# Layer normalisation on one core: variance and its root held once per token on a quarter of the partitions, then spread by four matmuls

## The reference, cut to what matters

```python
m = mean(x, axis=-1)
v = mean((x - m) ** 2, axis=-1)
y = (x - m) / sqrt(v + 1e-5)
```

## Time and profile before

| | us |
|---|---|
| median of 3 runs (4844.75 to 4852.0) | 4845.29 |
| the profiled execution, its own time | 4846.32 |
| its span in the profile | 4844.7 |
| PE busy | 4509.8 (93%) |
| DVE busy | 3645.8 (75%) |
| ACT busy | 3157.8 (65%) |
| POOL busy | 541.7 (11%) |
| mean granted TensorE clock | 0.962 |

### The profile page before, as it was taken

One profiled execution on the slowest core, in us unless ns is written; L12 is line 12 of the kernel. 1 busy time (PEld: TensorE's weight loads), 2 busy tenths in 40 slices (PEclk: granted clock), 3 DMA queues, 4 the chain that ended last, 5 costly groups with the idle time before them and its releaser, 6 DMA issues. The chain is left out here.

```text
span 4844.7 us, 107645 instructions
## 1 busy us (share of the span) xinstructions
PE 4509.8 (93%) x36227; PEld 2729.0 (56%) x36227; DVE 3645.8 (75%) x3699; ACT 3157.8 (65%) x5605; POOL 541.7 (11%) x1382
## 2 busy tenths in 40 slices
PE   6599999999999999999999969999885799999999
PEld 4344444444444444444444447777654478888887
DVE  4599999899999999999999956555355554444444
ACT  3158888788888888888888834444464454444444
POOL 4501111111111111111111100000000000000000
PEclk8789999999999999999999979999998899999999
DMA  5611110200202012012122220010001300000000
GB/s 174 190 29 21 24 28 18 34 18 18 34 18 34 19 21 35 18 31 65 39 56 45 44 88 28 25 35 9 27 17 48 123 14 9 13 13 13 13 4 14
DMA packets 217985, 182.41 MB, mean 38 GB/s; under 512 B 128032, under 2 KB 167632, under 8 KB 216448
## 3 DMA queue, kind: packets, MB, share of 16 engines
q1 hardware_dynamic: 201152, 167.99, 14.0%
q0 software_dynamic: 16384, 8.42, 0.7%
HBM read 120.47 MB, written 71.89 MB: 40 GB/s over the span
## 5 line engine op out<-in xcount | busy, mean ns | idle before, releaser
L894 DVE TENSOR_REDUCE PM<-A 128x2 f32<-128x1024 f32 x2092 | 2457.2, 1220 | 97.3 <-PE A L781 64.9
L871 ACT ACTIVATE PR<-SB 128x512 f32<-128x512 f32 x4100 | 2121.1, 603 | 367.2 <-PE SB L794 354.6
L814 PE MATMUL PV<-PR,VH 128*32 128x256 f32 x16384 | 1293.4, 387 | 3.5 <-issue 3.5
L781 PE MATMUL A<-QST,KA 48*128 48x512 f32 x4184 | 1196.4, 476 | 67.0 <-DMA QF<-QFD 40.8
L814 PEld LDWEIGHTS PV<-PR,VH 128*32 128x32 f32 x16384 | 433.2, 110 | 557.9 <-issue 367.0
L781 PEld LDWEIGHTS A<-QST,KA 48*128 48x128 f32 x4184 | 428.7, 187 | 525.1 <-issue 457.8
L794 PE MATMUL SB<-KST,QST 50*128 50x512 f32 x3075 | 689.8, 411 | 5.1 <-ACT PR L871 4.6
L794 PEld LDWEIGHTS SB<-KST,QST 50*128 50x128 f32 x3075 | 387.9, 187 | 213.3 <-ACT PR L871 209.3
L2045 DVE TENSOR_TENSOR m_h_lo<-m_h_full,m_h_hi 128x512 fp32r<-128x512 f32 x320 | 221.6, 693 | 276.5 <-ACT m_h_hi L1945 276.2
L802 PE MATMUL SB<-KF,QF 99*32 99x512 bf16 x4100 | 414.9, 384 | 1.2 <-ACT PR L871 1.2
L1939 ACT ACTIVATE m_h_full<-m_h,constants 128x512 f32<-128x512 f32 x320 | 219.6, 686 | 255.4 <-PE m_h L69 254.2
(11 more groups left out here) (280 smaller groups left out, 5503.6 us busy)
## 6 DMA issues: line engine op xcount, KB each, us to landing
QST<-QS SPq DMA_DIRECT2D x54, 256.0 KB, 9.0
KA<-KAD SPq DMA_DIRECT2D x402, 32.0 KB, 1.8
KST<-KS SPq DMA_DIRECT2D x402, 32.0 KB, 1.9
QS<-parts SPq DMA_DIRECT2D x16, 512.0 KB, 5.6
KS<-parts SPq DMA_DIRECT2D x16, 512.0 KB, 4.7
KAD<-dealt SPq DMA_DIRECT2D x16, 512.0 KB, 3.3
m_x<-X3T SPq DMA_DIRECT2D x16, 512.0 KB, 3.8
moe_w_lo<-W SPq DMA_DIRECT2D x16, 512.0 KB, 10.0
```

The lines of the kernel that those rows point to most:

```text
L781: return nc.tensor.matmul(A[:, u % 2 * 2 + e, :], keys, QST[rows, slot, j * TB:(j + 1) * TB], start=True, stop=True)
L814: mm = nc.tensor.matmul(PV[at:at + 2 * HD, 0:HB], VH[:, slot, e, c, :], PR[:, (2 * c + e) % P_SLOTS, b * HB:(b + 1) * HB], start=(c == 0), ...
L871: nc.scalar.activation(PR[:, v % P_SLOTS, :], SB[:, s_bank(v), :], ACT.Exp, scale=SCALE).then_inc(s_free, 1)
L894: nc.vector.tensor_reduce(PM[:, par, :, i, j:j + 1], A[:, u % 2 * 2:u % 2 * 2 + 2, :], AX.X, ALU.max).then_inc(a_free, 1)
```

## The change

The variance matmul is cut in four groups of 128 tokens. Group g uses only 32 columns of the matrix of 1/256 and writes partitions 32g to 32g+31, columns 0 to 127, of the bank. So one 128x128 tile holds the variances of all 512 tokens, each on 32 partitions. Root and reciprocal work on that tile. Four matmuls with a 128x128 selection (a column of `quarter`, which has a 1 at partition 32g, taken 128 times) then write the factor of each token to all partitions, over the same bank, and the scale reads it from PSUM. The new step (tensor_spread) needs a semaphore and a place in TensorE's order; in qkv0 and ffn0 other places move too.

```diff
-        self.std = self.sq[:, 0, :]
+        self.std = self.sq[:, 0, 0:P]
     def tensor_var(self, pe, i):
         pe.wait_ge(self.squared, count(i + 1))
         for k in range(KC):
-            mm = self.nc.tensor.matmul(self.var_ps, self.ones[:, :], self.sq[:, k, :],
-                                       start=(k == 0), stop=(k == KC - 1))
+            for g in range(TT):
+                rows = slice(g * P // TT, (g + 1) * P // TT)
+                mm = self.nc.tensor.matmul(self.var_ps[rows, 0:P], self.ones[:, 0:P // TT],
+                                           self.sq[:, k, g * P:(g + 1) * P], start=(k == 0), stop=(k == KC - 1))
         mm.then_inc(self.var_ready, 1)
+    def tensor_spread(self, pe, i):
+        pe.wait_ge(self.rstd_ready, count(i + 1))
+        for g in range(TT):
+            mm = self.nc.tensor.matmul(self.var_ps[:, g * P:(g + 1) * P], self.quarter[:, g:g + 1].to_broadcast([P, P]), self.std,
+                                       start=True, stop=True)
+        mm.then_inc(self.spread, 1)
-    def vector_reciprocal(self, dve, i, half):
+    def vector_reciprocal(self, dve, i):
         dve.wait_ge(self.std_ready, count(i + 1))
-        std = self.std[:, half * (TB // 2):(half + 1) * (TB // 2)]
-        self.nc.vector.reciprocal(std, std).then_inc(self.rstd_ready, 1)
+        self.nc.vector.reciprocal(self.std, self.std).then_inc(self.rstd_ready, 1)
     def vector_scale(self, dve, i):
-        dve.wait_ge(self.rstd_ready, count(i * 2 + 2))
-        rstd = self.std.unsqueeze(1).to_broadcast([P, KC, TB])
+        dve.wait_ge(self.spread, count(i + 1))
+        rstd = self.var_ps.unsqueeze(1).to_broadcast([P, KC, TB])
     def scalar_std(self, act, i, eps):
-        self.nc.scalar.activation(self.std, self.var_ps, ACT.Sqrt,
+        self.nc.scalar.activation(self.std, self.var_ps[:, 0:P], ACT.Sqrt,
...
# setup, POOL: quarter is one memset and one affine_select more
# qkv0, PE: spread between values 0 and values 1; ahead of the loop after turn(1)
-                    for pair in range(TT // 2):
-                        values(i, slot, pair)
+                    values(i, slot, 0)
+                    if following:
+                        ln.tensor_spread(pe, i + 1)
+                    values(i, slot, 1)
# qkv0, DVE
-                        for part in range(2):
-                            ln.vector_reciprocal(dve, i + 1, part)
-                        ln.vector_scale(dve, i + 1)
-                    low(i, slot, 3)
+                        ln.vector_reciprocal(dve, i + 1)
+                    low(i, slot, 3)
+                    if following:
+                        ln.vector_scale(dve, i + 1)
+                    values(i, 0)
                     if following:
                         ln.vector_lo(dve, i + 1, 1 - slot)
-                    values(i, 0)
                     values(i, 1)
# ffn0, PE, ACT, DVE (chunk: piece)
-  {9: "projection", 11: "mean", 14: "variance", 22: "gate"}
+  {9: "projection", 12: "mean", 16: "variance", 20: "spread", 25: "gate"}
-  {6: "o_hi", 13: "square", 15: "std", 20: "hi"}
+  {6: "o_hi", 15: "square", 18: "std", 22: "hi"}
-  10: "x1", 12: "centre", 16: "reciprocal0", 18: "reciprocal1", 19: "scale", 21: "lo", 23: "gate"
+  10: "x1", 13: "centre", 18: "reciprocal", 20: "scale", 22: "lo", 23: "gate"
# qkv1, PE: spread after queries/keys 3, ahead of the values
# out1, PE: spread of both slots after both variances; DVE: both reciprocals, then both scales
# moe, PE: spread at c == 21 (mean 12, variance 16 as before); DVE: one reciprocal at c == 19, scale at 22 as before
```

More of the change, by code:

```diff
@@ L253, in _ @@
                 nc.gpsimd.memset(K["eps"][:, :], EPS).then_inc(consts, 1)
-                pool.wait_ge(zeroed, 1)
+                nc.gpsimd.memset(K["quarter"][:, :], 0.0).then_inc(zeroed, 1)
+                pool.wait_ge(zeroed, 2)
                 nc.gpsimd.affine_select(out=ident[:, :], in_=ident[:, :], compare_op=ALU.not_equal,
@@ L257, in _ @@
                                         channel_multiplier=1).then_inc(consts, 1)
+                nc.gpsimd.affine_select(out=K["quarter"][:, :], in_=K["quarter"][:, :],
+                                        compare_op=ALU.not_equal, fill=1.0, base=0,
+                                        pattern=[[-(P // TT), TT]], channel_multiplier=1)
             @block.tensor
@@ L1115, in front @@
                         ln.tensor_var(pe, j)
+                    elif part == "spread":
+                        ln.tensor_spread(pe, j)
                     elif part == "gate":
@@ L1151, in blocks @@
                         if following:
-                            front(i + 1, 1 - slot, {9: "projection", 11: "mean", 14: "variance", 22: "gate"}.get(c))
-                for part in ("projection", "mean", "variance"):
+                            front(i + 1, 1 - slot, {9: "projection", 12: "mean", 16: "variance", 20: "spread",
+                                                             25: "gate"}.get(c))
+                for part in ("projection", "mean", "variance", "spread"):
                     front(0, 0, part)
@@ L1226, in front @@
                         ln.vector_centre(dve, j, slot)
-                    elif part in ("reciprocal0", "reciprocal1"):
-                        ln.vector_reciprocal(dve, j, int(part[-1]))
+                    elif part == "reciprocal":
+                        ln.vector_reciprocal(dve, j)
                     elif part == "scale":
@@ L1263, in blocks @@
                                 1: "den0", 2: "den1", 3: "den2", 4: "den3", 5: "quotient", 7: "o_lo",
-                                10: "x1", 12: "centre", 16: "reciprocal0", 18: "reciprocal1", 19: "scale",
-                                21: "lo", 23: "gate"}.get(c))
+                                10: "x1", 13: "centre", 18: "reciprocal", 20: "scale",
+                                22: "lo", 23: "gate"}.get(c))
                     dve.wait_ge(h_free, count((i + 1) * C + RING))
@@ L1287, in _ @@
                 weights.lo(dve, 1)
-                for part in ("reciprocal0", "reciprocal1", "scale"):
+                for part in ("reciprocal", "scale"):
                     front(0, 0, 0, part)
@@ L1435, in _ @@
                 ln.vector_centre(dve, 0)
-                for part in range(2):
-                    ln.vector_reciprocal(dve, 0, part)
+                ln.vector_reciprocal(dve, 0)
                 ln.vector_scale(dve, 0)
@@ L1655, in blocks @@
                     for s in SLOTS:
-                        for part in range(2):
-                            ln[s].vector_reciprocal(dve, i, part)
+                        ln[s].vector_reciprocal(dve, i)
+                    for s in SLOTS:
                         ln[s].vector_scale(dve, i)
```

39 lines of the change are left out of this document (24 added, 15 removed).

## The result

The changed kernel takes 4765.43 us (median of 5 runs, 4762.52 to 4768.82) against 4845.29 for the kernel before on the same chip: ratio 0.9829, 95% interval 0.9818 to 0.984. The profiled execution has a span of 4763.8 us against 4844.7.

| stage | before | after | measured | forecast |
|---|---|---|---|---|
| setup and qkv0 | 205.3 | 186.5 | -18.8 | -16 |
| attention | 2597.2 | 2589.6 | -7.6 | 0 |
| ffn0 | 660.2 | 638.0 | -22.2 | -13 |
| qkv1 | 146.3 | 133.4 | -12.9 | -2 |
| keys and values of the second attention | 46.7 | 47.1 | +0.4 | 0 |

A forecast was written before the change was run, and what follows sets the result against it. PE was taken to bound ffn0 and moe, a chain through the engines qkv0 and out1, with qkv1 between. Terms -16-13-2-19+0 = -50 from 4845.3 gave 4795 us, range 4783 to 4808 (8 in 10: 4776 to 4820).

The forecast's parts named there:

- the two kinds of price: Change priced as PE work in ffn0, qkv1 and moe, as chain length in qkv0, out1 and each stage's first block.
- small matmuls do overlap: Denies the rival that small matmuls don't overlap: variance 1.8 us, +1.05 on 20 PE-bound blocks, total 4820; chance 0.25.
- out1 keeps its clock of 0.77: Denies the rival that more clock comes back, in qkv0 and part of out1 (8 us more): 4781; chance 0.12.
- PE does not stand at the spread: Denies the rival that the spread blocks PE's in-order queue, 3 us in each of 28 blocks: slower, 4879; chance 0.05.
- only half the overlap: 1.2: Variance on 32-column weights: 1.2 us instead of 1.72, bounds 0.6 and 1.8.
- the net of a block: Block that PE bounds: spread 0.9, variance -0.5, change of width 0.1, net +0.5 us.
- the first chains: First blocks of qkv0, ffn0, qkv1, moe: one chain through reciprocal, root, variance and spread, -1.7 us each.
- the 0.55 that I gave it: Drains by the skill's rule: two per normalisation, at most 0.55 us per block, 11 us over 20 PE-bound blocks.
- 2.1 a block: ffn0: PE's waits for f_x and ln_lo go with the later places; -2.1+0.5 = -1.6 a block, stage -13.
- the wait of 5.2: qkv1: ln_lo wait of 7.0 us in 6 times, 5.2 of it once; 0.36 a block gained, +0.5 paid: 0.
- 4.9 sooner: out1: shorter reciprocals bring lo 0 4.9 us sooner; taken as -4.8 in each of 4 iterations, -19.
- moe 0 and qkv0 -16: moe: first chain -1.7, block 0 -1.3, six others +0.5 each, sum 0; qkv0: 7 x -2.0 -1.7 = -16.

The follow-up runs named there:

- variance_grouped: The changed kernel with the variance's two loops exchanged, so four instructions in a row go to the same quarter of the array; 4760.78 us.
- gate_later: The kernel before with one place moved: in ffn0 TensorE's gate from chunk 22 to 25; ratio 0.9979.
- places_only: The kernel before with the new places in ffn0 and qkv0 and none of the new operations; 4836.91 us, ratio 0.999.
- operations_only: The changed kernel with the places of before in ffn0 and qkv0; 4784.23 us, ratio 0.9873.
- out1_filled: The changed kernel with filler matmuls in out1, 4 behind the two variances and 12 behind the two spreads, each iteration; 4756.7 us, ratio 0.9817.

## Why the prediction was right and wrong

- **Direction and the two kinds of price**: right. The change pays as PE work in some stages and as a shorter chain in the others; reciprocal 0.95, scale unchanged and spread 0.9 held, the root took 0.37 instead of 0.27. The order of the stages did not hold: out1 was to give most and ffn0 gave most. The rivals fell: small matmuls do overlap (a block of moe takes 127.6 us instead of 127.7, where that rival wanted 1.5 more), out1 keeps its clock of 0.77, and PE does not stand at the spread where it is the bound (no wait of PE at all in ffn0's steady blocks).
- **"The two instructions of one fp32 matmul go to the same quarter, so I expect only half the overlap: 1.2"**: this step failed. Measured 0.58, just under the lower bound of 0.6: four instructions run at a time, the full overlap, and variance_grouped shows that the order of the quarters in the program has no part in it. With 0.2 around it instead of 0.1 the net of a block is -0.05, not +0.5: 20 blocks x 0.55 = 11 us of the 31 that were missing. The same term was wrong in the first chains, where I took 0.8 off the variance: in moe the root starts 1.15 us behind the variance's start instead of 3.82, in qkv1 0.7 instead of 3.0. On the change of width, the Trainium skill, "TensorEngine Tiling (Array Packing)", Key Properties, says that another tiling mode drains the engine; the 0.09 us ahead of the variance agrees with it in kind, and even with the 0.11 behind it the price is under half of the 0.55 that I gave it.
- **"PE stands 1.3 us for f_x and 0.8 for ln_lo: 2.1 a block"**: mis-sized, since I took the idle figure for the price. By gate_later a wait costs 0.27 more, twice a block, 7 blocks: 4 us in ffn0. In qkv1 I also took the wait of 5.2 for the main part of the earlier trace rows and the short ones, 0.2 to 0.4 each, for small; each costs 0.4 to 0.6 from start to start and they are gone: the period went from 15.5 to 14.7. 0.8 x 7 = 6. Of the other 7 us of qkv1 the first stretch, to the first reciprocal, has 3.9 (variance from 3.0 to 0.7, root 0.3, and, by chance, a load that landed 1.3 sooner: this stretch, 14.8 before, is 14.1 and 15.7 in gate_later and places_only), the rest the shorter chains of the first and the last normalisation.
- **Attention, "I let it only shift"**: put at 0 because it has no normalisation. The stage is 54% of the span; its steps answer to the place of the code (4.6 us of the 7.6), and nothing in the rows of before could have told that.
- **"out1: 4.9 sooner"**: 3.2 to 3.7 measured (from first reciprocal to first reciprocal 31.9, 31.4, 30.1 before and 28.8, 27.9, 26.4 after). The spreads were taken as 0.9 each; at half clock they take 1.9, so scale starts 3.1 us behind the first reciprocal instead of the 2.0 that the prediction's times give. The price at half clock stood in the prediction; the stage's sum didn't use it.
- **moe 0 and qkv0 -16**: moe's first chain gave 3.2 instead of 1.7 us and block 0 2.9 instead of 1.3, the other six the 0.55 above. In qkv0 the mechanism (low 3 in the time of the spread, part of the clock back) came as described, -18.8; places_only shows that the same order without the short reciprocal loses 10.7. That the sum comes within 3 us says little of its terms, since the stage scatters by 3 from kernel to kernel.
- **The size as a whole**: the misses of ffn0 (9), qkv1 (11), moe (6.5), attention (8) and qkv0 (3) point the same way, and out1's 6 the other.

## What to carry to other kernels

Read a wait of TensorE from start to start and not from the idle figure, and add what the first matmul behind it takes longer. When a change adds or removes instructions, compare the stages that it does not touch before crediting it with the sum: here 4.6 us of 80 came from the place of the code; 40 idle matmuls took them off the kernel before as well and put 14 us on the ninth and tenth steps of the changed one. Read a time that agrees with its forecast stage by stage as well: in operations_only and in out1_filled the sum was right and the terms were not. Try the places and the operations of a change apart: an order that pays with the new operations can lose without them.

## What was unexpected

- 16 fp32 instructions with 32-wide weights and 128 columns take 0.58 us, and another 16 behind them 0.43, in both orders of the quarters that were tried: four start within 20 to 40 ns, the next four 0.11 us later. 8 with 128-wide weights take 0.80.
- TensorE stops for 1.3 to 2.6 us at fixed steps of a loop, and 40 matmuls more ahead of the loop made such stops vanish in one kernel and appear in another.
- Matmuls that nobody reads made out1 10.4 us shorter (124.8 to 114.4) at a granted clock of 0.92 instead of 0.77.
